# Third graph layer: POOL waits for the row buffer by quarters of a chunk

## The reference

```python
def _L2_gnn_ref(x, edge_idx, W_l, W_r, att, bias):     # the third layer, H = 6 heads
    gl = (x @ W_l).reshape(n, H, F_OUT)
    gr = (x @ W_r).reshape(n, H, F_OUT)
    s = jax.nn.leaky_relu(gl[src] + gr[dst], NEG_SLOPE)
    e = jnp.einsum('ehf,hf->eh', s, att)
    m = jax.ops.segment_max(e, dst, num_segments=n)
    p = jnp.exp(e - m[dst])
    denom = jax.ops.segment_sum(p, dst, num_segments=n)
    alpha = p / (denom[dst] + 1e-16)
    msg = alpha[:, :, None] * gl[src]
    out = jax.ops.segment_sum(msg, dst, num_segments=n)
...
edge_index = jnp.stack([src, dst])
x = _layernorm(x + _L0_gnn_ref(x, L0_gnn_weight, src, dst, edge_type_16), axis=-1)
x = _layernorm(x + _L1_gnn_ref(x, L1_gnn_beta, src, dst), axis=-1)
x = _layernorm(x + _L2_gnn_ref(x, edge_index, L2_gnn_W_l, L2_gnn_W_r, L2_gnn_att, L2_gnn_bias), axis=-1)
x = _layernorm(x + _L3_gnn_ref(x, L3_gnn_W, L3_gnn_coeff, L3_gnn_h_bias, L3_gnn_loop_weight, src, dst, edge_type_8), axis=-1)
```

## Time and profile before

| | |
|---|---|
| median of 3 timed runs | 6202.34 us |
| lowest and highest | 6194.47 and 6212.94 us |
| the profiled execution | 6149.63 us, span 6147.8 us |
| busy, share of the span | POOL 57%, DVE 47%, PE 26%, ACT 18% |
| granted TensorE clock, mean | 0.615 |
| third layer's chunks | from 3005 us to 4720 us of the span |

### The profile page before, as it was taken

How to read it: one execution, slowest core, us unless ns; L and a number is a source line. 1 busy time by engine, 2 the same in 40 slices (tenths; PEclk the granted TensorE clock), 3 DMA queues, 4 the chain that set the end, 5 groups by cost and what they waited for, 6 DMA issues and landing times.

```text
span 6147.8 us, 31588 instructions
## 1 busy us (share of the span) xinstructions
PE 1595.5 (26%) x6543; PEld 813.1 (13%) x6543; DVE 2871.9 (47%) x7562; ACT 1115.1 (18%) x3419; POOL 3520.1 (57%) x3636
## 2 busy tenths in 40 slices
PE   5531110000000000002375566666664500000002
PEld 1421110000000000001122222222221400000001
DVE  2344444125354455544255565555556632444344
ACT  1100000000000000001155555555555400000000
POOL 5355666766666666664634544454442576676754
PEclk7765555555555555556687888888887655555555
DMA  4212222221222222221123333333334221222222
GB/s 140 105 53 62 65 67 72 72 67 61 51 72 65 64 70 72 69 67 37 49 103 122 140 139 129 125 140 139 129 124 157 67 67 54 65 79 76 67 68 72
DMA packets 185944, 529.62 MB, mean 86 GB/s; under 512 B 70454, under 2 KB 75170, under 8 KB 169480
## 3 DMA queue, kind: packets, MB, share of 16 engines
q1 hardware_dynamic: 65816, 395.51, 17.0%
q0 software_dynamic: 117696, 129.81, 10.5%
q10 hardware_dynamic: 2224, 2.13, 0.1%
HBM read 185.57 MB, written 341.44 MB: 86 GB/s over the span
## 4 chain that ended last, share of the span: by engine, by line
DVE 39%; another core or an unknown queue 24%; issue 18%; PE 11%; ACT 5%; POOL 3%; DMA 1%; DVEq 0%; ACTq 0%; POOLq 0%; SPq 0%
DVE AR L1673 10%; DVE AR L514 5%; DVE ps L779 5%; PE ps L1220 4%; POOL AR L190 2%; PE ps L1236 2%; DVE AR L850 2%; DVE AR L1385 2%; ACT AR L1371 2%; DVE AR L364 1%; DVE AR L1663 1%; ACT AR L1227 1%; DVE AR L800 1%; PE ps L680 1%
## 5 line engine op out<-in xcount | busy, mean ns | idle before, releaser
L190 POOL DMA_INDIRECT AR<-xt,Si x2496 | 2402.0, 962 | 1687.3 <-issue 743.9
L190 POOL DMA_INDIRECT AR<-y,R x752 | 721.4, 959 | 520.9 <-issue 222.2
L1385 DVE SCALAR_TENSOR_TENSOR AR<-AR,gf 128x390 f32<-128x390 f32 x780 | 484.2, 621 | 654.3 <-ACT AR L1371 458.3
L1220 PE MATMUL ps<-AR,WLR 128*128 128x512 f32 x1248 | 681.7, 673 | 131.6 <-ACT AR L1227 88.2
L1673 DVE SCALAR_TENSOR_TENSOR AR<-AR,gf 128x128 f32<-128x128 f32 x831 | 295.0, 355 | 472.6 <-DVE AR L1673 360.1
L1371 ACT ACTIVATE AR<-AR 128x64 f32<-128x64 f32 x1664 | 495.5, 346 | 0.0
L1227 ACT ACTIVATE AR<-ps 128x512 f32<-128x512 f32 x624 | 368.5, 591 | 210.9 <-remote 146.7
L779 DVE SCALAR_TENSOR_TENSOR ps<-ps,gf,AR 128x64 f32<-128x64 f32 x831 | 242.2, 291 | 303.5 <-remote 160.5
L514 DVE SCALAR_TENSOR_TENSOR AR<-AR,gf 128x64 f32<-128x64 f32 x831 | 237.5, 286 | 258.2 <-DVE AR L514 155.5
L190 POOL DMA_INDIRECT AR<-s,endi x196 | 215.5, 1100 | 186.8 <-issue 112.4
L1220 PEld LDWEIGHTS ps<-AR,WLR 128*128 128x128 f32 x1248 | 238.8, 216 | 436.7 <-issue 312.5
(11 more groups left out here) (324 smaller groups left out, 2987.6 us busy)
## 6 DMA issues: line engine op xcount, KB each, us to landing
s<-AR SPq DMA_DIRECT2D x51, 3168.0 KB
AR<-xd SPq DMA_DIRECT2D x104, 512.0 KB
s<-AR SPq DMA_DIRECT2D x51, 1024.0 KB
AR<-xt,Si POOLq DMA_INDIRECT x2496
s<-AR SPq DMA_DIRECT2D x53, 512.0 KB
s<-AR SPq DMA_DIRECT2D x51, 528.0 KB
xd<-AR SPq DMA_DIRECT2D x52, 512.0 KB
y<-AR SPq DMA_DIRECT2D x24, 1024.0 KB
```

The lines of the kernel that those rows point to most:

```text
L190: g.indirect_dma_start(out=o, out_offset=None, in_=table, in_offset=bass.IndirectOffsetOnAxis(ap=idx, axis=0)).then_inc(S[sem], 16)
L1220: t.matmul(PS[2 + k % 3][:], WLR[:, ch * P:(ch + 1) * P], XT2[:, u % 6, :], start=True, stop=True).then_inc(S["pm"], 1)
L1385: m = v.scalar_tensor_tensor(out=Sv[:, j, 0:HW], in0=Sv[:, j - 1, 0:HW], scalar=gf[:, c * CH + j:c * CH + j + 1], in1=Sv[:, j, 0:HW], op0= ...
```

## The change

POOL no longer waits once, ahead of a chunk's 16 gathers, until both ACT and DVE have done with the whole buffer. It waits ahead of each four gathers, until ACT and DVE have done with the four rows that these will overwrite: for `p2` at the second, fourth, sixth and eighth pair of rows, and for `ap` at the 9th, 17th, 25th and 33rd piece. The last pair of waits is the one that stood ahead of the chunk before. The gathers, their order and their semaphores are the same.

```diff
         def g2_chunk(e, c):
-            if c >= NX:
-                e.wait_ge(S["p2"], p2_end(c - NX))
-                e.wait_ge(S["ap"], 33 * (c - NX + 1))
             for j in range(CH):
+                if c >= NX and j % 4 == 0:
+                    e.wait_ge(S["p2"], p2_end(c - NX) - 6 + j // 2)
+                    e.wait_ge(S["ap"], 33 * (c - NX) + 1 + 2 * (j + 4))
                 gather(xsv(c)[:, j, 0:D], xt2, Si[:, c * CH + j:c * CH + j + 1], f"g_{2 * (c % NX) + j // 8}")
```

## The result

The changed kernel took 5912.33 us (median of 4, 5905.27 to 5918.31) beside 6198.41 us for the kernel before (6193.02 to 6212.94): ratio 0.9535, 95% interval 0.9513 to 0.9556. The profiled execution took 5918.3 us, its span is 5916.5 us, 231.3 less than before.

A forecast was written before the change was run, and what follows sets the result against it. Long runs of POOL's gathers were taken to stall PE and ACT in the third layer, 32.3 us a chunk; cutting them to 29.0 over 47 chunks saves 155 us: 6202 - 155 = 6047 us, range 5860 to 6265.

The forecast's parts named there:

- likeliest case: Third layer's periods of 27 to 31 us a chunk, so 6140 to 5953 us in all; chance 0.48.
- No direct gain, 40 us of slack: POOL's gathers are first read by PE over 40 us later, so issuing them sooner feeds nobody sooner: gain nothing.
- The waits cost nothing: Six more POOL waits a chunk, at most 2.4 us, are hidden by POOL's idle 12.7 us; taken as nothing.
- The stall comes with gathers and not with the store: Third layer: PE's signals arrive slowly in long gather runs; 15 us a chunk lost; the store alone isn't the cause.
- The stall holds until the run's end and 3.1 us more: PE and ACT stay slowed, at 0.13 of full speed, until 3.1 us behind the end of POOL's gather run.
- A run is harmless for 8.4 us and a pause clears the charge: PE and ACT slow only after 8.4 us of unbroken gathers; a POOL pause of 4.42 us clears most of it.
- The walk to 27.6 us, and 29 taken: One steady-state chunk with four runs of 5 us gives a period of 27.6 us; 29 taken since pauses are short.
- The sum: Third layer: (32.3 - 29.0) x 47 chunks = 155 us off the median of 6202, giving 6047 us.
- hidden anyway: Rival: slowing of PE and ACT goes with the number of gathers, not their grouping; 6202 us, chance 0.18.
- the Trainium skill's rule: A DMA never contends with a compute engine, and PE and ACT never wait on anyone; by it 6202 us.
- A stall in every run: Rival: up to four slowed ends of gather runs a chunk, not one; 6249 to 6912 us, chance 0.22.
- POOL becomes the bound: Rival: 5 us runs never slow PE and ACT; period 20.0 or 22.4 us, 5624 to 5737 us, chance 0.07.

The follow-up runs named there:

- six gathers: Kernel before, one wait a chunk, but only the first three gathers of each half made from the sixth chunk on: 5570.93 us in one run.
- a small store: Kernel before, but SP writes only the first of a chunk's sixteen columns of sums (198 KB in place of 3168 KB): 32.5 us a chunk in the third set.
- the set at 4816 us: Second set, kernel before at 4816.14 us; eight gathers 4747.91, one column stored 5328.12, quarter-length rows 4826.90, changed kernel with runs of at most six gathers 5321.11 us.
- halves: Changed kernel, but POOL waits ahead of each eight gathers for that half's release, not each four: 5966.71 us beside 6202.86, ratio 0.9615.

## Why the prediction was right, and where it was not

- *The time*: 5912 us lies inside the range of 5860 to 6265, but below the likeliest case of 5950 to 6140, which got 0.48. The direction and the kind of gain were right; the size came out larger.
- *No direct gain, 40 us of slack*: right. The kernel with one wait half a chunk later spends 11 us of that slack and is faster for it.
- *The waits cost nothing*: nearly. Alone they cost 0.4% (0.2 to 0.6). The idle time that was to hide them is 11.8 us a chunk (544.9 us in 46 waits from 3150 to 4645 us); the 12.7 holds the one wait of 51.7 us of the earlier trace rows.
- *The stall comes with gathers and not with the store*: right wherever before takes over 6000 us: six gathers 19.6 us a chunk, a small store 32.5. But the set at 4816 us shows that it needs more than gathers.
- *The stall holds until the run's end and 3.1 us more*: right in kind, but the tail is 1.3 to 2.3 us.
- *A run is harmless for 8.4 us and a pause clears the charge*: this is the step that failed. Even its size was misread: in the earlier trace rows ACT's wait begins at 3617.12 - 2.77 = 3614.35, 7.3 us behind the run's first gather, so the two onsets seen were 6.4 and 7.3 us. Behind the run's first gather the onset lies at 6.6, 9.1, 13.0 or 13.9 us, by kernel; in the chunk it lies between 4.4 and 9.3 us. So it goes by what PE and ACT are at more than by the length of the run. What is seen: in the kernel before the run ends some 21 us into the chunk, so that the stall can last from 7.2 to 23.5; with quarters, halves or a later wait it ends some 12 us into it, and the stall lasts from some 5 to 14. The rest of the run falls where nothing stalls. That the trigger is PE's 32 products at L1236, of which some run just ahead of each onset looked at, I only argue.
- *The walk to 27.6 us, and 29 taken*: measured 26.95. The walk has a run of 4 and an unbroken one of 12, and a stall of 9.7 us that begins 8.4 us behind the first gather of the 12. The trace has a run of 4 and one of 12 too (the last two quarters of a buffer and the first of the next, where the walk has the last three of one), and a stall of 8.4 us that begins 9.1 us behind. So the walk itself came near, and the 29 taken in its place made the forecast worse: (32.3 - 27.6) x 47 would be 221 us. That its rule for the onset gave nearly the right number for this kernel is luck, as the halves and the later wait have 13.0 and 13.9 us.
- *The sum*: 6047.2 against 5912.3, 135 us. Of these the periods are 93: (32.34 - 26.95) x 46 = 248 us in place of 155. The span fell by 231 and not by 248, as the first L1329 came 30.2 us later (3133.93 against 3103.71), which is ahead of any edited wait, and the rest was 13 us shorter: 17 us the other way. The distance of the median to the profiled execution was 52.7 us above for before, and is 6.0 below for after: 59 us. The first is the term that was mis-sized; the last should have been left out, as one execution says little of how another stands to its median.
- *The rivals*: "hidden anyway" fell; and so, in the sets over 6000 us, did the Trainium skill's rule (SBUF — State Buffer, Who interferes with whom) as the prediction used it, as a rule on time: ACT's long waits go when ten of the sixteen gathers go. Whether it holds for SBUF's ports no run here shows. In the set at 4816 us the traces agree with it. "A stall in every run" did not come: there is one a chunk, and none beside the run of four (PE is busy for all of 3732 to 3736, at a granted clock of 0.50). "POOL becomes the bound" came only in that other set, at 20.9 to 21.2 us a chunk.

## What to carry to other kernels

When engines stand idle with nothing that the trace can name, look for another engine's burst that ends just ahead of their going on, and try to move that burst before you cut it: here one later wait gave a period of 27.1 us where four finer ones gave 27.0, out of slack that was there. And time the kernel before again in each set: it moved from 6203 to 4816 us, more than by any edit here, and what an edit is worth may move with it.

## What the runs showed of the hardware

- Beside a run of indirect gathers PE, ACT and DVE stood still together, for 7 to 14 us a chunk by ACT's idle time, and went on 1.3 to 2.3 us behind its last gather, whatever the store beside it (3168 or 198 KB a chunk). In the longest wait of one chunk ACT went on 9.4 us behind the modelled end of PE's products.
- None of four kernels of one set had such a stall, two of them beside endless gathers of POOL, and the kernel before, not profiled there, was 22% shorter (4816 against 6203 us).
- A gather issued behind others landed late enough that a wait for it cost POOL 3.9 us on average, up to 8.9, in the set at 4816 us.
- A pause of PE of 6.1 us (3751.99 to 3758.05) was followed by a granted clock of 0.50 to 0.54 from 3758 to 3764 us.
